# SwitchHead output gates: rows repeated from DRAM into 64 partitions and multiplied in place, instead of spread by TensorE products

## The chip, the cores and the metric

One core of a Trainium2 chip runs the whole program as one launch. The metric is the device time of that launch in microseconds (us). Engines are called by the names of the profile: PE (TensorE), PEld (its weight loads), DVE (VectorE), ACT (ScalarE), POOL (GpSimd) and SP, whose queue issues nearly all DMA transfers.

## What is computed

Four layers run one after the other on an input of 4 x 1024 x 128: two Mamba layers, SwitchHead attention with an FFN, a narrow attention, and a mixture of experts. The change is in the second. Its reference, cut to what matters (here H = 16 heads, P = 64, E = 8 experts, K = 2, D = 128; after the input is replaced, the batch is 4 and the length 1024):

```
def _gate(x, Wsel):
    s = jax.nn.sigmoid(jnp.einsum('bsd,hed->bhse', x, Wsel))
    _, idx = jax.lax.top_k(s, K)
    mask = jax.nn.one_hot(idx, E, dtype=s.dtype).sum(-2)
    return s * mask

q = _rope(einsum('bsd,hdp->bhsp', x, Wq)); k = _rope(einsum('bsd,hdp->bhsp', x, Wk))
gv = _gate(x, Wsel_v)
v = einsum('bsd,bhse,hedp->bhsp', x, gv, Wv)
att = softmax(einsum('bhsp,bhtp->bhst', q, k) / sqrt(P))
o = einsum('bhst,bhtp->bhsp', att, v)
go = _gate(x, Wsel_o)
return einsum('bhsp,bhse,hepd->bsd', o, go, Wo)
```

The last line is what the change is about: for each head and each of its 8 experts, the head's output `o` (64 features, transposed, so features lie on partitions) is multiplied by that expert's gate, one number for each position, and then by that expert's 64 x 128 matrix.

## The kernel before

**Tiling.** Heads go in pairs: 4 batches x 8 pairs = 32 pairs, and each pair in two halves of 512 positions. Head 0 of the pair lies on partitions 0 to 63, head 1 on 64 to 127. The work of a pair is spread over 8 "turns", so that the stage has 64 x 4 = 256 turns and some more at its end.

**A turn.** `turn` writes the steps of all engines in one list; every engine runs through this list in order and does its own part of each step, with semaphores between the engines. Turn m (d = m % 8) holds for PE: two `col` steps (transposed scores of this pair, which ACT turns into exponentials), two `row` steps (scores of the next pair, of which DVE takes the maximum), `bcast`, two `values` steps (products of the exponentials with V), at times `sums` (column sums of the exponentials, added up before on POOL) and `qk` (the projection of the pair after next, in turns d = 0 and 2), `onto`, one piece of the next batch's gates or of the FFN of the batch before (`ahead`: `prelude`, `ffn`, in the last batch `tables` and `decay`), at times `max_t`, and `v` (the value projection, which DVE multiplies by the value gates and sums over experts). DVE ends a turn with `recip`, a reciprocal of a quarter of the sums.

**PSUM.** The steps of PE that other engines read share a ring of three slots of 128 x 1024 in the order of the list: a step waits until the slot used three ring steps before has been read.

**The output gates.** `gate_t` transposes the gates of 512 positions to one row for each head and expert. ACT and DVE split them into three bf16 parts (`gate_mid`, `gate_res`, `gate_lo`), `gate_store` writes them to DRAM, and with `out_weights` SP brings the 16 rows of the pair, three parts, back twice into the tile `GS` (48 of each 64 partitions). `bcast` (L1387 to L1395) multiplies a constant selection matrix `selg` by `GS`: two products of 48 x 128 with 48 x 512, bf16, put the gates of two experts for both heads onto 128 partitions in PSUM. DVE multiplies this 128 x 1024 (L1727) by `OT`, the scaled output of the half, into `OG`, of which there are two; `onto` (L1404) multiplies `OG` by the experts' matrices and adds up in PSUM (`Z`); after four such steps, `collect` (L1740) adds `Z` to the batch's output. Unit x, one of 256 (half and expert pair), is in `bcast` in turn x + 9 and in `onto` in turn x + 10.

**`OT`** is made on POOL (L1944) at the end of turns d = 0 and 4, out of the head output that ACT has copied and the reciprocals. POOL also adds up the exponentials (L1953, L1956: seven additions of 128 x 1024 in four turns, two in most turns), does the rotary products of `qk` (L1918, after a transfer that swaps rows, and L1924), and parts of the search for the two largest gates (`top_a` to `top_d`) and of the FFN's affine steps.

**The end.** After the last `col` the remaining `values`, `sums`, `bcast` and `onto` steps follow one another closely, and `last_ffn` is woven in. One of its first steps is `d_load`, with which SP loads the first operands of the next layer.

Of the kernel before, what the change touches and what calls it, by code (L numbers as in the profile page):

```python
# [12 lines left out]
NB = 4  # L13
# [813 lines left out]
class SwitchHead:  # L827
    NORMS = 4

    def __init__(self, nc, ctx, room, c, W):  # L830
# [13 lines left out]
        self.selg = sb("selg", [128, 8, 128], BF16)  # L844
# [9 lines left out]
        self.GS = [sb(f"GS{u}", [128, L], BF16) for u in range(2)]  # L854
# [5 lines left out]
        self.OG = [sb(f"OG{u}", [128, 2, 512]) for u in range(2)]  # L860
# [12 lines left out]
        self.gt_d = dram("s_gt", (2, 3, 128, L), BF16)  # L873
# [5 lines left out]
        self.RG = self.TT[:, 0:512]  # L879
# [7 lines left out]
        ring = ("rows", "gate", "gate_t", "qk", "v", "row", "max_t", "col", "sums", "bcast", "f_t", "f_rows",  # L887
# [6 lines left out]
        for name in ("consts_in", "selg_in", "selg_done", "zeroed", "ln_chain", "ln_out", "top_v", "own_top", "b2_done", "spill_out", "top_done", "gt_hi",  # L894
                     "gt_mid", "gt_res", "gt_lo", "gates_out", "gv_out", "raw_done", "swap_in", "turn_done",
                     "rope_done", "wq_in", "wv_in", "gvj_in", "v_done", "mm_done", "m_s", "m_v", "m_in", "values_done",
                     "add_done", "o_done", "recip_done", "ot_done", "gs_in", "wo_in", "onto_done", "outt_done", "wf_in", "xn_in", "aff_done",
                     "t_in", "t_s", "t_v", "ij_in", "d_f", "d_hi", "d_mid", "d_lo", "d_res"):
            self.__setattr__(name, ctx.enter_context(nc.semaphore("s_" + name)))

# [48 lines left out]
    def turn(self, m, rows, vs, ahead):  # L949
# [15 lines left out]
        if due(self.BCAST):  # L965
            h, e = part(self.BCAST)
            out.append(("bcast", *self.of_half(h), e))
# [6 lines left out]
        h, x = part(self.SUMS)  # L974
        if due(self.SUMS) and x == 0:
            out.append(("sums", *self.of_half(h)))
# [12 lines left out]
        if due(self.SUMS):  # L989
            out.append(("recip", *self.of_half(h), x))  # L990
# [146 lines left out]
    def sync(self, sp):  # L1137
# [5 lines left out]
        sp.dma_start(self.M1[:, 0:16], W["s_selg"]).then_inc(self.selg_in, 16)  # L1143
        sp.wait_ge(self.zeroed, 7)
        for step in self.steps:
# [6 lines left out]
            elif kind == "gate_store":  # L1152
                if b > 1:
                    sp.wait_ge(self.gs_in, 96 * 8 * (b - 1))
                sp.wait_ge(self.gt_lo, 2 * (b + 1))
                for p in range(3):
                    sp.dma_start(self.gt_d[b % 2, p], self.GT[:, p, :]).then_inc(self.gates_out, 16)
# [41 lines left out]
            elif kind == "out_weights":  # L1199
                j, k = step[2], self.turns(*step[1:])  # L1200
                if k > 1:
                    sp.wait_ge(self.onto_done, 8 * (k - 1))
                    r.taken(sp, ("bcast", *self.pair(k - 2), 1, 3))
                if k:
                    sp.wait_ge(self.wo_in, 16 * k)
                    sp.wait_ge(self.gs_in, 96 * k)
# [4 lines left out]
                sp.wait_ge(self.gates_out, 48 * (b + 1))  # L1211
                for p in range(3):
                    for at in (16 * p, 64 + 16 * p):
                        sp.dma_start(self.GS[j % 2][at:at + 16, :],
                                     self.gt_d[b % 2, p, 16 * j:16 * j + 16, :]).then_inc(self.gs_in, 16)
            elif kind == "f_load":
                if b + 2 < NB:
                    sp.wait_ge(self.gates_out, 48 * (b + 3))
                    r.filled(sp, ("gate_t", b + 2, 1))
# [72 lines left out]
    def tensor(self, pe):  # L1292
        c, r, n = self.c, self.r, self.n
        for step in self.steps:
# [3 lines left out]
            if kind == "consts":  # L1298
                pe.wait_ge(self.consts_in, 16 * 5)
                pe.wait_ge(self.selg_done, 1)  # L1300
                pe.wait_ge(self.zeroed, 7)
# [156 lines left out]
    def scalar(self, s):  # L1458
        c, r, n = self.c, self.r, self.n
        for step in self.steps:  # L1460
# [18 lines left out]
            elif kind == "consts":  # L1479
                s.wait_ge(self.selg_in, 16)  # L1480
                s.activation(self.selg[:, :, :].rearrange("p e (h m) -> p (e h) m", h=2), bcast(self.M1[:, 0:16], 64),
                             ACT.Copy).then_inc(self.selg_done, 1)
                s.wait_ge(self.consts_in, 16 * 5)
                s.wait_ge(self.zeroed, 7)
# [11 lines left out]
            elif kind == "gate_t":  # L1496
                r.filled(s, step)
                if b > 0:
                    s.wait_ge(self.gates_out, 48 * b)
                s.activation(self.GT[:, 0, 512 * j:512 * j + 512], ps[:, 0:512], ACT.Copy).then_inc(self.gt_hi, 1)  # L1500
            elif kind == "gate_mid":
                r.taken(s, ("gate_t", b, j))
# [1540 lines left out]
```

## Time and profile before

| what | value |
|---|---|
| median of 3 runs | 5604.74 us (5603.9 to 5605.07) |
| time of the profiled execution | 5603.34 us |
| its span in the profile | 5601.5 us |
| PE busy | 5008.6 us (89%) |
| DVE busy | 4141.8 us (74%) |
| POOL busy | 2670.9 us (48%) |
| ACT busy | 2434.5 us (43%) |
| granted PE clock, mean | 0.965 of full |
| bytes moved by DMA | 340.14 MB |

The busy times are shares of the whole span, over stages with different limits. The stage of this change runs from about 1023 us (the end of Mamba) to 3945 us. Instructions are pipelined, so that the distance from one start to the next says more than a duration does.

### The profile page before, as it was taken

The numbers are of one execution on the slowest core, as the hardware profiler recorded it, in microseconds if no ns is written. First come the engines' busy times: TensorE is split into PE (matmuls) and PEld (weight loads), VectorE is DVE, ScalarE is ACT, GpSimd is POOL, SyncE is SP. The second block draws the span as 40 slices with busy tenths as digits, with TensorE's granted clock in tenths as the row PEclk, the third lists the DMA queues.
The fourth block names the chain that finished last, engine by engine and source line by source line (L and its number), as shares of the span: only waits on it lengthen the run. The fifth ranks groups of instructions, "written<-read, shape, count | busy, mean of one in ns | idle before, by whom it ended". The sixth has DMA issues, their size and how long they took to land.

```text
span 5601.5 us, 69295 instructions
## 1 busy us (share of the span) xinstructions
PE 5008.6 (89%) x23700; PEld 1998.6 (36%) x23738; DVE 4141.8 (74%) x4659; ACT 2434.5 (43%) x2991; POOL 2670.9 (48%) x1431
## 2 busy tenths in 40 slices
PE   7898998699999999999999999999788888888756
PEld 3333333233333333433334333433333322222225
DVE  5889989777777777677776787675777788888721
ACT  5655555133222323323233222332356656777753
POOL 4887888466655665556655555554211110110015
PEclk9999999899999999999999999999799999999978
DMA  4555555210110101101011011011121111011005
GB/s 149 180 188 180 188 190 191 72 38 23 36 33 23 30 24 42 33 23 30 23 44 33 24 35 34 23 42 21 45 42 41 36 22 30 24 29 19 2 12 177
DMA packets 137560, 340.14 MB, mean 61 GB/s; under 512 B 31867, under 2 KB 48766, under 8 KB 136564
## 3 DMA queue, kind: packets, MB, share of 16 engines
q1 hardware_dynamic: 134216, 329.40, 19.8%
q0 software_dynamic: 3008, 6.32, 0.3%
q8 instruction: 204, 3.34, 0.2%
q14 instruction: 132, 1.08, 0.1%
HBM read 289.59 MB, written 35.04 MB: 58 GB/s over the span
## 4 chain that ended last, share of the span: by engine, by line
PE 37%; issue 8%; DVE 4%; ACT 3%; POOL 1%; SPq 0%; POOLq 0%; DMA 0%; ACTq 0%; DVEq 0%
PE ps L2310 7%; PE ps L1377 4%; PE ps L1404 4%; PE ps L1362 3%; PE ps L1349 3%; PE ps L2281 3%; PE ps L1340 3%; PE ps L2263 3%; ACT n_P L2368 2%; DVE n_MX L2446 1%; PE ps L1366 1%; PE ps L2710 1%; PE ps L2721 1%; PE ps L2214 1%; PE ps L1333 1%
## 5 line engine op out<-in xcount | busy, mean ns | idle before, releaser
L2446 DVE TENSOR_REDUCE n_MX<-ps 128x2 f32<-128x1024 f32 (+7 forms) x1040 | 980.0, 975 | 223.5 <-PE ps L2263 128.8
L1956 POOL TENSOR_TENSOR s_PA<-s_PA,shared 128x1024 f32<-128x1024 f32 x384 | 908.8, 2367 | 318.0 <-ACT shared L1532 290.2
L1532 ACT ACTIVATE shared<-ps 128x1024 f32<-128x1024 f32 x512 | 522.1, 1022 | 1127.0 <-PE ps L1366 1114.6
L2368 ACT ACTIVATE n_P<-ps 128x1024 f32<-128x1024 f32 (+4 forms) x1021 | 823.0, 838 | 401.5 <-PE ps L2281 210.6
L767 POOL TENSOR_TENSOR m_PR<-m_HH,m_CS 128x1024 f32<-128x1024 f32 x256 | 606.0, 2383 | 162.5 <-issue 146.9
L1698 DVE TENSOR_REDUCE s_MX<-ps 128x2 f32<-128x1024 f32 x512 | 592.7, 1201 | 5.0 <-PE ps L1349 4.7
L1690 DVE TENSOR_TENSOR XTB<-ps,s_GVJ 128x1024 f32<-128x1024 f32 x256 | 312.9, 1222 | 358.6 <-PE ps L1340 356.6
L1349 PE MATMUL ps<-s_QF 64*128 64x512 f32 x2048 | 500.8, 606 | 71.5 <-DVE XTB L1690 44.7
L1362 PE MATMUL ps<-s_QF 64*128 64x512 f32 x2048 | 553.5, 617 | 6.9 <-DVE s_MX L1698 4.7
L2310 PE MATMUL ps<-n_P,n_VA 128*32 128x512 f32 (+3 forms) x3584 | 518.6, 577 | 17.4 <-ACT n_P L2368 17.0
L544 PE MATMUL ps<-m_PR,ident 128*128 128x512 f32 x1024 | 506.3, 622 | 11.0 <-DVE m_ZS L736 6.4
L1404 PE MATMUL ps<-s_OG,s_WO 128*128 128x512 f32 x1024 | 501.9, 612 | 0.7 <-DVE s_OUTT L1740 0.5
L1377 PE MATMUL ps<-shared,s_V 128*64 128x512 f32 x2048 | 496.8, 606 | 0.0
L1340 PE MATMUL ps<-s_WV,XTB 128*128 128x512 f32 x1024 | 482.7, 594 | 1.3 <-DVE XTB L1690 0.8
L730 DVE TENSOR_TENSOR_SCAN m_HH<-m_DA,ps 128x1024 f32<-128x1024 f32 x176 | 402.5, 2287 | 6.6 <-ACT m_DA L666 0.6
L1727 DVE TENSOR_TENSOR s_OG<-ps,s_OT 128x1024 f32<-128x1024 f32 x256 | 311.1, 1215 | 90.8 <-issue 60.8
L1918 POOL TENSOR_TENSOR s_TA<-s_TA,s_CS 128x1024 f32<-128x1024 f32 x64 | 151.3, 2364 | 472.8 <-DMA s_TA<-XTB 472.8
L2493 POOL TENSOR_TENSOR ln_small<-ln_small,n_half 128x8 f32<-128x8 f32 x11 | 18.1, 1648 | 641.0 <-DVE ln_small L2405 641.0
L1692 DVE TENSOR_REDUCE s_V<-XTB 128x128 f32<-128x1024 f32 x256 | 312.4, 1220 | 8.8
L1349 PEld LDWEIGHTS ps<-s_QF 64*128 64x128 f32 x2048 | 200.8, 190 | 303.7 <-issue 274.1
L1404 PEld LDWEIGHTS ps<-s_OG,s_WO 128*128 128x128 f32 x1024 | 178.1, 189 | 307.8 <-issue 304.6
L1362 PEld LDWEIGHTS ps<-s_QF 64*128 64x128 f32 x2048 | 177.4, 186 | 290.6 <-issue 285.1
(372 smaller groups left out, 7102.4 us busy)
## 6 DMA issues: line engine op xcount, KB each, us to landing
m_CS<-m_rows_c SPq DMA_DIRECT2D x256, 512.0 KB
m_BS<-m_rows_c SPq DMA_DIRECT2D x80, 512.0 KB
s_WV<-in_s_v SPq DMA_DIRECT2D x32, 512.0 KB, 3.7
s_TA<-XTB SPq DMA_DIRECT2D x256, 64.0 KB, 2.3
s_WO<-in_s_o SPq DMA_DIRECT2D x32, 512.0 KB, 3.9
g_WB<-in_g_wx SPq DMA_DIRECT2D x23, 578.0 KB
n_parts<-n_PT SPq DMA_DIRECT2D x14, 768.0 KB, 3.3
shared<-n_parts SPq DMA_DIRECT2D x144, 64.0 KB
```

Of the source, the lines that this page charges most:

```text
L767: g.tensor_tensor(self.PR[n % 4][:, :], self.HH[n % 4][:, :], self.CS[n % self.NCS][:, :], ALU.mult).then_inc(self.prod_done, 1)
L1340: ins = pe.matmul(ps[:, q], self.xt(b)[:, t * 128:(t + 1) * 128], self.WV[:, q], start=True, stop=True)
L1349: ins = pe.matmul(ps[:, 512 * h:512 * h + 512], QF[hs, 0, t * 128:(t + 1) * 128], QF[hs, 1, 512 * q:512 * q + 512], start=True, stop=True)
L1362: pe.matmul(ps[:, 512 * h:512 * h + 512], QF[hs, 1, t * 128:(t + 1) * 128], QF[hs, 0, qs], start=True, stop=False)
L1377: ins = pe.matmul(self.O[64 * h:64 * h + 64, :], self.V[j % 2][:, h, t, :], self.P[g % 4][:, 512 * h:512 * h + 512], start=t == 0, stop=t ...
L1404: ins = pe.matmul(self.Z, self.WO[j % 2][:, 2 * e + i, :], self.OG[e % 2][:, i, :], start=e == i == 0, stop=e == 3 and i == 1)
L1532: s.activation(self.P[g % 4], ps, ACT.Exp).then_inc(*r.take(step))
L1698: v.tensor_reduce(self.MX[:, q, :, t], ps.rearrange("p (h n) -> p h n", h=2), AX.X, ALU.max, negate=True).then_inc(*r.take(step))
L1956: g.tensor_tensor(PA, PA, P, ALU.add).then_inc(self.add_done, 1)
L2310: ins = pe.matmul(ob[at:at + 32, lo - 512 * q:512], self.VA[s % 3][:, t, 8 * g + 2 * hp + hh, :], self.P[(32 * n + 8 * hp + t) % 3][q][:, ...
L2368: ins = s.activation(P[:, at:at + x.shape[1], lo:512], x[:, :, lo:512], ACT.Exp, scale=scale)
L2446: ins = v.tensor_reduce(self.MX[:, q, at:at + x.shape[1], hp, t], x[:, :, 0:width], AX.X, ALU.max)
```

## The change

- The gate rows are kept as one f32 row for each head and expert (`GTF`, in the place of `GT`). `gate_t` is copied by ACT alone; the splitting into three parts, with `gate_mid`, `gate_res` and `gate_lo`, is gone, and so are `selg`, `GS` and their setup.
- A new step `gate_in`, one for each unit x, in turn x + 7 behind `onto`: SP loads for each of the two heads the two rows of 512 gates, repeated onto 64 partitions, into `OG` itself, of which there are now three (NG = 3). Before that it waits until `onto` x - 3 is done.
- The two products of `bcast` are gone, and the step leaves the PSUM ring. In its place in the list stands `gated`: `OG` is multiplied by `OT` in place, on DVE for even x (even expert pairs, odd turns) and on POOL for odd x (even turns).
- `onto` waits for the one or the other, and POOL's `OT` step for both.

```diff
@@ order
-            out.append(("bcast", *self.of_half(h), e))
+            out.append(("gated", *self.of_half(h), e))
...
         if due(self.BCAST + 1):
             ho, eo = part(self.BCAST + 1)
             out.append(("onto", *self.of_half(ho), eo))
             if eo == 3:
                 out.append(("collect", *self.of_half(ho)))
+        if 0 <= m - self.BCAST + 2 < 64 * NB:
+            h, e = part(self.BCAST - 2)
+            out.append(("gate_in", *self.of_half(h), e))
...
     def gate_pieces(self, b, r):
-        for kind in ("gate_t", "gate_mid", "gate_res"):
-            self.out.append((kind, b, r))
-            yield
-        self.out.append(("gate_lo", b, r))
+        self.out.append(("gate_t", b, r))
+        yield
@@ SP
+            elif kind == "gate_in":
+                j, q, e = step[2:]
+                x = 4 * self.half(b, j, q) + e
+                if x >= self.NG:
+                    sp.wait_ge(self.onto_done, x - self.NG + 1)
+                sp.wait_ge(self.gates_out, 16 * (b + 1))
+                for h in range(2):
+                    at = 16 * j + 8 * h + 2 * e
+                    src = self.gt_d[b % 2, at:at + 2, 512 * q:512 * q + 512]
+                    sp.dma_start(self.OG[x % self.NG][64 * h:64 * h + 64, :, :],
+                                 src.partition_broadcast(64)).then_inc(self.og_in[x % self.NG], 16)
@@ SP, out_weights
-                sp.wait_ge(self.gates_out, 48 * (b + 1))
-                for p in range(3):
-                    for at in (16 * p, 64 + 16 * p):
-                        sp.dma_start(self.GS[j % 2][at:at + 16, :],
-                                     self.gt_d[b % 2, p, 16 * j:16 * j + 16, :]).then_inc(self.gs_in, 16)
@@ PE
-            elif kind == "bcast":
-                q, e = step[3:]
-                pe.wait_ge(self.gs_in, 96 * (self.turns(b, j) + 1))
-                r.empty(pe, step)
-                for i in range(2):
-                    rows = slice(64 * i, 64 * i + 48)
-                    ins = pe.matmul(ps[:, 512 * i:512 * i + 512], self.selg[rows, 2 * e + i, :],
-                                    self.GS[j % 2][rows, 512 * q:512 * q + 512], start=True, stop=True)
-                ins.then_inc(*r.fill(step))
@@ PE, onto
-                r.taken(pe, ("bcast", *step[1:]))
+                x = 4 * self.half(b, j, q) + e
+                pe.wait_ge(self.og_g if e % 2 else self.og_v, x // 2 + 1)
...
-                    ins = pe.matmul(self.Z, self.WO[j % 2][:, 2 * e + i, :], self.OG[e % 2][:, i, :],
+                    ins = pe.matmul(self.Z, self.WO[j % 2][:, 2 * e + i, :], self.OG[x % self.NG][:, i, :],
@@ DVE
-                v.tensor_tensor(self.OG[e % 2][:, :, :], ps.rearrange("p (i n) -> p i n", i=2),
-                                self.OT[k % 2][:, :].unsqueeze(1).to_broadcast([128, 2, 512]),
-                                ALU.mult).then_inc(*r.take(step))
+            elif kind == "gated" and step[4] % 2 == 0:
+                self.gated(v, step, self.og_v)
...
+    def gated(self, e, step, done):
+        k = self.half(*step[1:4])
+        x = 4 * k + step[4]
+        OG = self.OG[x % self.NG][:, :, :]
+        e.wait_ge(self.og_in[x % self.NG], 32 * (x // self.NG + 1))
+        e.wait_ge(self.ot_done, k + 1)
+        e.tensor_tensor(OG, OG, self.OT[k % 2][:, :].unsqueeze(1).to_broadcast([128, 2, 512]), ALU.mult).then_inc(done, 1)
@@ POOL
+            elif step[0] == "gated" and step[4] % 2:
+                self.gated(g, step, self.og_g)
```

## Rows read from the trace of the kernel before

**Rows 1.** Busy time by stretch of the stage: engines, granted PE clock, DMA share, GB/s.
```profile
1612.00:2314.00 702.00, 694.16 (x2716) 275.18 (x2714) 512.39 (x529) 206.41 (x266) 395.55 (x195) 1.00 0.11 30
...
3885.00:3911.00 26.00, 23.49 (x66) 8.11 (x64) 19.04 (x34) 4.33 (x8) 2.53 (x2) 1.00 0.51 78
3911.00:3946.00 35.00, 17.26 (x110) 14.90 (x112) 16.43 (x62) 12.78 (x35) 0.23 (x1) 0.90 0.00 1
```

**Rows 2.** Timeline of PE in a turn: start us, us, engine line, out<-in.
```profile
2421.55 1.88 PE L1349 MATMUL ps<-s_QF 64*128 64x512 f32 x8
2423.26 0.39 PE L1394 MATMUL ps<-s_GS,s_selg 48*128 48x512 bf16 x2
2423.58 1.94 PE L1377 MATMUL ps<-shared,s_V 128*64 128x512 f32 x8
```

**Rows 3.** Timeline of PE in a turn before the first gate product.
```profile
1196.46 1.88 PE L1349 MATMUL ps<-s_QF 64*128 64x512 f32 x8
...
1198.28 1.94 PE L1377 MATMUL ps<-shared,s_V 128*64 128x512 f32 x8
```

**Rows 4.** Part 5 of the page: DVE's multiplications by value gates and output gates.
```profile
L1690 DVE TENSOR_TENSOR XTB<-ps,s_GVJ 128x1024 f32<-128x1024 f32 x256 | 312.9, 1222 | 358.6 <-PE ps L1340 356.6
...
L1727 DVE TENSOR_TENSOR s_OG<-ps,s_OT 128x1024 f32<-128x1024 f32 x256 | 311.1, 1215 | 90.8 <-issue 60.8
```

**Rows 5.** Timeline of all engines, turn 1 of a pair (2431 to 2442 us).
```profile
2432.78 2.35 POOL L1918 TENSOR_TENSOR s_TA<-s_TA,s_CS 128x1024 f32<-128x1024 f32 x1 [7.57 <-DMA s_TA<-XTB]
...
2438.75 4.85 POOL L1956 TENSOR_TENSOR s_PA<-s_PA,shared 128x1024 f32<-128x1024 f32 x2
2438.89 1.23 DVE L1727 TENSOR_TENSOR s_OG<-ps,s_OT 128x1024 f32<-128x1024 f32 x1 [2.41 <-issue]
...
2440.03 0.68 DVE L1740 TENSOR_TENSOR s_OUTT<-s_OUTT,ps 128x512 f32<-128x512 f32 x1
...
2441.54 1.23 DVE L1690 TENSOR_TENSOR XTB<-ps,s_GVJ 128x1024 f32<-128x1024 f32 x1 [0.83 <-PE ps L1340]
...
2443.68 1.88 PE L1349 MATMUL ps<-s_QF 64*128 64x512 f32 x8
```

**Rows 6.** Timelines of POOL, DVE and PE, turn 5 of the same pair.
```profile
2477.24 4.86 POOL L1956 TENSOR_TENSOR s_PA<-s_PA,shared 128x1024 f32<-128x1024 f32 x2
...
2478.41 1.22 DVE L1708 TENSOR_TENSOR s_MM<-s_MX 128x16 f32<-128x16 f32 x1 [0.23 <-DVE s_MX L1698]
2479.55 1.21 DVE L1727 TENSOR_TENSOR s_OG<-ps,s_OT 128x1024 f32<-128x1024 f32 x1
...
2483.35 1.23 DVE L1690 TENSOR_TENSOR XTB<-ps,s_GVJ 128x1024 f32<-128x1024 f32 x1
...
2485.50 1.88 PE L1349 MATMUL ps<-s_QF 64*128 64x512 f32 x8
```

**Rows 7.** Timelines: DVE with two SBUF inputs, POOL idle and POOL working.
```profile
1087.77 0.17 DVE L1708 TENSOR_TENSOR s_MM<-s_MX 128x16 f32<-128x16 f32 x1
...
3312.08 12.22 POOL L1956 TENSOR_TENSOR s_PA<-s_PA,shared 128x1024 f32<-128x1024 f32 x4
...
3315.55 6.54 DVE L1824 SCALAR_TENSOR_TENSOR Y<-Y 128x1024 f32<-128x1024 f32 x2
```

**Rows 8.** Timelines of DVE and PE, a turn 1 that carries a search piece.
```profile
1311.36 2.80 DVE L1627 TENSOR_TENSOR s_TG<-s_TG,s_M 128x512 f32<-128x512 f32 x1
...
1315.44 1.99 PE L1349 MATMUL ps<-s_QF 64*128 64x512 f32 x8 [2.74 <-DVE XTB L1690]
```

**Rows 9.** DMA issues: size of each, median us from issue to landing.
```profile
s_WO<-in_s_o SPq DMA_DIRECT2D x32, 512.0 KB, 3.9
```

**Rows 10.** Timeline of PE and SP at the end of the stage.
```profile
3884.95 1.98 PE L1404 MATMUL ps<-s_OG,s_WO 128*128 128x512 f32 x4
...
3887.26 8.21 SPq L824 DMA_DIRECT2D shared<-n_parts  x24
...
3908.54 1.96 PE L1404 MATMUL ps<-s_OG,s_WO 128*128 128x512 f32 x4 [0.17 <-DVE s_OG L1727]
```

More of the change, by code:

```diff
@@ L828 @@
     NORMS = 4
+    NG = 3
     def __init__(self, nc, ctx, room, c, W):
@@ L859, in __init__ @@
         self.OT = [sb(f"OT{u}", [128, 512]) for u in range(2)]
-        self.OG = [sb(f"OG{u}", [128, 2, 512]) for u in range(2)]
+        self.OG = [sb(f"OG{u}", [128, 2, 512]) for u in range(self.NG)]
         self.PA = [sb(f"PA{u}", [128, L]) for u in range(2)]
@@ L886, in __init__ @@
         self.O, self.Z = PS[:, 3072:3584], PS[:, 3584:4096]
-        ring = ("rows", "gate", "gate_t", "qk", "v", "row", "max_t", "col", "sums", "bcast", "f_t", "f_rows",
+        ring = ("rows", "gate", "gate_t", "qk", "v", "row", "max_t", "col", "sums", "f_t", "f_rows",
                 "f_up", "f_down", "d_rows", "d_qk", "d_qk2", "d_v")
@@ L973, in turn @@
                     out.append(("keep", *self.pair(k), i // 8))
-        h, x = part(self.SUMS)
+        hs, x = part(self.SUMS)
         if due(self.SUMS) and x == 0:
-            out.append(("sums", *self.of_half(h)))
+            out.append(("sums", *self.of_half(hs)))
         if d in (0, 2):
@@ L1152, in sync @@
             elif kind == "gate_store":
-                if b > 1:
-                    sp.wait_ge(self.gs_in, 96 * 8 * (b - 1))
-                sp.wait_ge(self.gt_lo, 2 * (b + 1))
-                for p in range(3):
-                    sp.dma_start(self.gt_d[b % 2, p], self.GT[:, p, :]).then_inc(self.gates_out, 16)
+                for u in range(self.NG if b > 1 else 0):
+                    sp.wait_ge(self.og_in[u], 32 * len(range(u, 64 * (b - 1), self.NG)))
+                for x in range(2):
+                    r.taken(sp, ("gate_t", b, x))
+                sp.dma_start(self.gt_d[b % 2], self.GTF).then_inc(self.gates_out, 16)
+            elif kind == "gate_in":
[9 more added lines that the diff above has]
+                                 src.partition_broadcast(64)).then_inc(self.og_in[x % self.NG], 16)
             elif kind == "gv_store":
@@ L1210, in sync @@
                     sp.dma_start(c.slots[at, :], W["g_blank"]).then_inc(c.blank, 16)
[L1211 to L1215 removed]
             elif kind == "f_load":
                 if b + 2 < NB:
[L1218 to L1219 removed]
+                    sp.wait_ge(self.gates_out, 16 * (b + 3))
                     sp.wait_ge(self.top_done, self.tops(b + 2))
@@ L1498, in scalar @@
                 if b > 0:
[L1499 to L1502, printed above, removed]
-                s.activation(self.GT[:, 1, 512 * j:512 * j + 512], self.RG, ACT.Copy).then_inc(self.gt_mid, 1)
-            elif kind == "gate_lo":
-                s.wait_ge(self.gt_res, 2 * b + j + 1)
-                s.activation(self.GT[:, 2, 512 * j:512 * j + 512], self.RG, ACT.Copy).then_inc(self.gt_lo, 1)
+                    s.wait_ge(self.gates_out, 16 * b)
+                s.activation(self.GTF[:, 512 * j:512 * j + 512], ps[:, 0:512], ACT.Copy).then_inc(*r.take(step))
             elif kind == "qk":
@@ L1544, in scalar @@
                 r.filled(s, step)
-                if j == 0 and b + 2 < NB:
-                    s.wait_ge(self.gt_res, 2 * (b + 3))
                 s.activation(self.TT[:, j % 2 * 256:(j % 2 + 1) * 256], ps[:, 0:256], ACT.Copy).then_inc(*r.take(step))
@@ L1900, in gpsimd @@
         self.own_p = own = Own(g, self.c.own_g)
-        for u in range(2):
-            g.memset(self.GS[u][:, :].bitcast(F32), 0.0).then_inc(self.zeroed, 1)
         g.memset(self.TA[:, 1, :], 0.0).then_inc(self.zeroed, 1)
@@ L1942, in gpsimd @@
                 if k > 1:
-                    self.r.taken(g, ("bcast", *self.pair((k - 2) // 2), k % 2, 3))
+                    g.wait_ge(self.og_v, 2 * (k - 1))
+                    g.wait_ge(self.og_g, 2 * (k - 1))
                 g.tensor_tensor(self.OT[k % 2][:, :], self.OR[k % 2][:, 0, :], self.OR[k % 2][:, 1, :],
```

49 lines of the change are left out of this document (11 added, 38 removed).

## The prediction

> **What bounds the kernel now.** I read three views, in this order. First the busy time by stretch over the stage that the change touches [rows 1]: between 1612 and 3885 us TensorE (PE) is busy 99% of the time at the full granted clock, VectorE (DVE) 73%, GpSimd (POOL) 56%, the DMA engines 11%. The reader is to see that what leaves PE's queue shortens the stage, and that the other engines matter only where PE waits for them. Second, PE's timeline inside a turn, for what a piece costs from start to start; the mean durations in the groups overlap and overstate it. Third, the timelines of DVE, POOL and SP beside PE's, for the slack between each engine and the PE instruction that waits for it. The stage is 256 turns of 9.8 to 11.5 us.
>
> **PE: what goes.** With a gate product, the score rows ("row") start at 2421.55, the gate product at 2423.26 and the value products at 2423.58: 2.03 us from rows to values [rows 2]. Before the first gate product of the phase the same step takes 1198.28 - 1196.46 = 1.82 us [rows 3]. So one turn is worth 0.21 us, not the 2 x 378 ns that two products seem to take. Of 256, nine stand in the tail, which I price as a whole below: 247 x 0.21 = 52 us. Behind it in a ring of three PSUM slots, `row` still takes the slot that the last `v` of the turn before used, three places back as now; no slot gets tighter.
>
> **Small pieces.** The splitting of the gate rows into three bf16 parts (two copies on ScalarE and two subtractions on DVE each, eight times) goes, and so do DVE's multiplications of the even-numbered turns (half of 256, 1215 ns each, [rows 4]), which relieves DVE there. PE waits there only rarely; with the shorter start of the phase I allow 7 us of gain (0 to 12).
>
> **The new multiplications on POOL.** 128 of them, about 2.4 us each (half of the 4.85 us of two additions, [rows 5]). They fall in turns 0, 2, 4 and 6 of eight. In turn 0 POOL stands idle 7.57 us for the rotary swap's DMA [rows 5], which covers one; PE asks for the product a turn later. Cost nothing there; if that cover went, `ot` (the scaled head output) would be late.
>
> **The new multiplications on DVE.** Here is the main cost. Today the operand comes from PSUM. Afterwards both inputs are in SBUF. What such an instruction meets while POOL works is shown [rows 7]: the minimum of two 128x16 tiles takes 0.17 us with POOL idle, but 1.22 us at 2478.41 [rows 6], ending just as POOL's first addition does; and at 3315 two `scalar_tensor_tensor` take 6.54 us while POOL's four additions stretch to 12.22 us. They take turns, one whole instruction each. So a DVE multiplication waits for the POOL instruction in progress. DVE waits for PE before the `v` multiplication for 356.6 us in all, 1.4 a turn [rows 4]; in turns 3 and 7, with nothing else to do, for longer, and that covers it. Turns 1 and 5 carry more:
>
> Turn 1 [rows 5]: POOL starts its additions at 2438.75, the moment `ot` is done; DVE comes at 2438.89. It would wait to 2441.2 and end at about 2442.3 instead of 2440.12. Then come the collect (0.6 from start to start) and the `v` multiplication (1.23), which ends at 2444.1; PE's next row needs it. That row stands at 2443.68 and would come 0.21 earlier, 2443.47; with a handover of 0.1 (at 1311.36 DVE's 2.80 plus one `v` of 1.2 end at 1315.3, and PE starts at 1315.44, [rows 8]) PE loses 0.7 us. Bounds 0.4 to 0.9. 32 pairs: 22 us.
>
> Turn 5 [rows 6]: the 128x16 instruction slips in between POOL's two additions, and the multiplication follows at 2479.55 while POOL's second is due at 2479.65. If POOL gets in first, DVE waits to 2482.1 and ends at 2483.2, 2.4 later than now; 0.75 of that is idle today, so `v` ends 1.7 later, at 2486.3, against 2485.29 for PE: 1.0 us lost. If DVE gets in first, nothing or 0.3. The two are 0.1 us apart; in [rows 7] POOL always got in between two DVE instructions, but these waited for one another and this pair doesn't. I take the middle, 0.65: 21 us (5 to 32).
>
> The Trainium skill ("SBUF — State Buffer", Who interferes with whom) states the lock as a rule: a DVE instruction with two SBUF inputs contends with a GpSimd instruction that reads SBUF, and whichever starts first keeps the port for its whole length. The traces agree with the first half; by the second half alone DVE, which starts 0.1 us sooner, would win in turn 5, and the sum would be 16 us lower: that is the first rival.
>
> **Turns that also carry the top-2 search, the FFN or the tables.** PE already stalls there: 2.74 us before 1315.44, behind a DVE instruction of half the size that POOL held to 2.80 us [rows 8]. The later multiplication adds about 0.4 in such a turn 1 and 0.6 in a turn 3 (six each) and some in the table stretch: 8 us (3 to 18, as POOL has little left there).
>
> **SP's queue.** `gate_in` waits for the `onto` of its own turn, so SP now walks beside PE. Behind it stand the swap transfers, the maxima's six small transfers and the weights, each of which waits today for something of about the same place. A 512 KB load lands 3.9 us after issue [rows 9]; `gate_in` has some 17 us until its multiplication. 256 x 512 KB is 134 MB, 50 GB/s more on engines that are 11% busy. Nothing, in the steady part.
>
> **The tail is different.** Once the columns end (3884.95 to the last `onto` at 3908.54 plus 1.9, [rows 10]) each `gate_in` waits for the `onto` three back, then 4.3 us to land, then 1.2 (DVE) or 2.4 us (POOL), then 1.8 for `onto`: about 9 us for three. The loads of the next phase (`d_load`, 30 transfers, 24 of them in 8.21 us, 10.3 in all [rows 10]) stand between the last two `gate_in`s in SP's order. Counting from the end of the `onto` at 3884.95 (number 246 of 0 to 255) at 3886.9: load 249 issues at 0.1, lands at 4.4, POOL is done at 6.8 and `onto` 249 at 8.7. Load 250 issues after `onto` 247 (2.9) and its `onto` ends at 10.5; load 251, after `onto` 248 (5.5), lands at 9.8, POOL 12.2, `onto` 14.1. Loads 252 to 254 so issue at 8.8, 10.6 and 14.2, and `onto` 252, behind `ot`, a collect and four transposes, ends at 18.2. `d_load` then runs to 25.2; load 255 lands at 29.5, is multiplied to 32, and its `onto` ends at 33.7, against 23.5 today. 10 us, and as PE would be half busy for as long as from 3911 to 3946, where the granted clock was 0.90 [rows 1], 3 more: 13 us (6 to 20).
>
> The Trainium skill ("SBUF — State Buffer", Door 1: The DMA port swizzle) says that a transfer onto 64 partitions reaches only half the SBUF ports, and that two of them serialize. By its 196 GB/s an estimate for the two halves is 2.7 us of transfer, which would put some 1 to 2 us on a landing and about 4 us on the tail; no row here shows such a transfer.
>
> **Sum.** -52 - 7 + 22 + 21 + 8 + 13 = +5 us. The profiled execution took 5603.34 (span 5601.5), 1.4 under the median 5604.74. 5603.3 + 5 = 5608. A change of 0.2%, 11 us, is about what a measurement of this kernel tells from none; so I forecast no measurable change: PE's gain is given back by waits for DVE.
>
> **Rivals.**
>
> *The lock hardly reaches PE (faster).* DVE wins turn 5 (5 instead of 21), and turn 1 costs 0.4 (13): -52 - 7 + 13 + 5 + 5 + 10 = -26, 5577. For it: the 0.1 us lead at 2479.55. Against it: POOL's start at 2438.75 is plain, and turn 1's slack is only some 0.8 us.
>
> *POOL always first, and POOL short of time (slower).* Turn 5 at 32 us, turn 1 at 26, the search turns at 18, the tail at 17, relief 3: -52 - 3 + 26 + 32 + 18 + 17 = +38, 5641. The mechanism is one, the port shared by DVE and POOL; it decides from about 1.9 us of PE stall in eight turns, where the 1.7 us saved are gone (the rest being the tail). For it: the alternation at 3312, and POOL, which would be busy nearly all of turns 0 to 3 during the search.
>
> *The rows come late in every turn (much slower).* If a `gate_in` were held behind another wait of SP for more than some 13 us, PE would stand at each `onto`; at 0.3 us in each of 256 turns 77 us, 5680. Against it: none of SP's waits, ordered as PE runs, is that long.
>
> *The products cost PE nothing, so that nothing is gained (slower too).* Against it: [rows 2, 3]. I give it no more than 0.02, inside the slower ones.
>
> **Chances.** No measurable change 0.33; first rival 0.32; slower by the lock 0.29; slower by late rows or otherwise 0.06. Faster by over 0.2%: 0.32; within: 0.33; slower: 0.35. Range for 8 in 10: from 5574 (first rival with its bounds) to 5640; the likeliest case's own is 5593 to 5616.
>
> **What would show it.** In the changed profile: no matmul from the gate rows, rows to values 1.82 us; DVE's multiplications with a mean near 2 us instead of 1.215, those of turn 1 ending 3.5 us after `ot`; PE stalls of some 0.5 to 1 us before the `row` of turns 2 and 6, some 60 of them, put down to the `v` multiplication; POOL's multiplications near 2.4 us; the last `onto` about 34 us after the columns end, behind a `gate_in` issued after the 24 loads. I am wrong if stalls appear at `onto` itself in the steady part (rows late), if DVE's mean stays at 1.2 us (no lock), or if turns 2 and 6 start on time.

## The result, and the profile after

The changed kernel takes 5641.68 us (median of 4 runs, 5634.91 to 5650.98) beside 5604.90 (4 runs of before, 5603.90 to 5613.09): a ratio of 1.0064, 95% interval 1.005 to 1.0079. That is 37 us slower, 34 over the predicted 5608, and 1.7 above the upper end of the range. The profiled execution, the fastest of the four, took 5634.91, span 5633.1, which is 31.6 over the span of before; I account for those 31.6.

The page and the windows first: groups of part 5 that answer to [rows 4], and two issues that answer to [rows 9].

```profile
L1663 DVE TENSOR_TENSOR XTB<-ps,s_GVJ 128x1024 f32<-128x1024 f32 x256 | 312.2, 1220 | 316.1 <-PE ps L1341 315.0
L1745 DVE TENSOR_TENSOR s_OG<-s_OG,s_OT 128x1024 f32<-128x1024 f32 x128 | 297.1, 2321 | 118.0 <-POOL s_OT L1920 110.5 <-DMA s_OG<-s_gt 7.5
L1745 POOL TENSOR_TENSOR s_OG<-s_OG,s_OT 128x1024 f32<-128x1024 f32 x128 | 308.9, 2414 | 33.3 <-DMA s_OG<-s_gt 33.3
...
s_OG<-s_gt SPq DMA_DIRECT2D x512, 256.0 KB, 3.9
...
s_WO<-in_s_o SPq DMA_DIRECT2D x32, 512.0 KB, 5.1
```

DVE's new multiplication takes 2.32 us in the mean where 1.2 is its own work, as forecast; POOL's takes 2.41. A transfer of gate rows lands 3.9 us after its own issue. Each multiplication needs two, of which the second is issued 0.6 us behind the first, and the pair has landed 4.75 us after the first issue (median of the 256 pairs), where I took 4.3. The neighbouring weights land 1.2 us later than before, and no wait of PE is put down to them. By stretch [rows 1]:

```profile
1612.00:2314.00 702.00, 683.17 (x2579) 266.52 (x2579) 517.47 (x507) 205.82 (x260) 490.96 (x228) 0.99 0.28 75
...
3910.00:3978.00 68.00, 26.26 (x125) 17.88 (x124) 22.13 (x80) 14.63 (x40) 3.63 (x2) 0.77 0.26 45
```

PE is busy 97% of the middle of the stage where it was 99%; POOL went from 56% to 70%, the DMA engines from 11% to 28%. The end of the stage has become 68 us in which PE mostly stands, at a granted clock of 0.77.

**Where the 31.6 us are.** In both traces I take from PE's timeline the start of the value products of every turn, 250 starts, of which the last lies at the end of the columns; then the start of the next phase's first product (out of `shared`); then the end of the span.

| | before | after | difference |
|---|---|---|---|
| the last of these value products starts at | 3878.98 | 3884.81 | +5.8 |
| from there to the next phase's first product | 66.8 | 93.6 | +26.8 |
| from there to the end of the span | 1655.7 | 1654.7 | -1.0 |

The first line contains -2.8 from ahead of the first of these turns (in the ten kernels below it is between -2.3 and +0.6, so no more than a fluctuation need be in it). Of the 249 intervals behind it 160 are shorter by 0.19 to 0.24 us. The others differ by what PE waits in them; most are longer, but 24 are shorter by more than that, up to 3.0 us, since before had a wait there too. Counting 0.215 for each of the 249 as gained (53.5 in all), PE's waits cost 62.2 us more than they did before. By the place of the turn in its eight, this net cost lies so:

| turn | 1 | 3 | 5 | the other five |
|---|---|---|---|---|
| us lost, sum over all pairs | 30.3 | 20.5 | 4.5 | 6.9 |

A blocked multiplication is not yet a loss: in turn 7, one of the other five, DVE's takes 2.8 us in 28 of the 32 pairs, and PE loses 3.6 us there in all.

**Turn 1**, the pair of [rows 5], in the timelines of POOL, DVE and PE after:

```profile
2438.30 8.14 POOL L1932 TENSOR_TENSOR s_PA<-s_PA,shared 128x1024 f32<-128x1024 f32 x3
...
2438.45 3.28 DVE L1745 TENSOR_TENSOR s_OG<-s_OG,s_OT 128x1024 f32<-128x1024 f32 x1 [2.43 <-POOL s_OT L1920]
2441.65 0.68 DVE L1706 TENSOR_TENSOR s_OUTT<-s_OUTT,ps 128x512 f32<-128x512 f32 x1
2442.25 1.21 DVE L1663 TENSOR_TENSOR XTB<-ps,s_GVJ 128x1024 f32<-128x1024 f32 x1
...
2443.61 1.99 PE L1350 MATMUL ps<-s_QF 64*128 64x512 f32 x8 [0.43 <-DVE XTB L1663]
```

POOL starts its additions 0.15 us ahead of DVE, DVE waits one whole addition out, and the `v` multiplication behind it ends 0.15 before PE's late row. The interval is 0.70 longer than a stall-free one would be: the predicted 0.7.

**Turn 5** of the same pair [rows 6]:

```profile
2476.61 5.73 POOL L1932 TENSOR_TENSOR s_PA<-s_PA,shared 128x1024 f32<-128x1024 f32 x2
...
2477.78 1.23 DVE L1681 TENSOR_TENSOR s_MM<-s_MX 128x16 f32<-128x16 f32 x1 [0.23 <-DVE s_MX L1671]
2478.93 1.21 DVE L1745 TENSOR_TENSOR s_OG<-s_OG,s_OT 128x1024 f32<-128x1024 f32 x1
...
2483.14 1.21 DVE L1663 TENSOR_TENSOR XTB<-ps,s_GVJ 128x1024 f32<-128x1024 f32 x1
...
2484.65 1.88 PE L1350 MATMUL ps<-s_QF 64*128 64x512 f32 x8
```

The multiplication takes its bare 1.21 us right behind the 128x16 instruction, and it is POOL that waits: its two additions take 5.73 us instead of 4.86. PE doesn't wait. The Trainium skill's rule ("SBUF — State Buffer", Who interferes with whom: the one that starts first holds the port for its whole instruction) fits both turns.

**The end of the stage** [rows 10], the timelines of SP, POOL and PE:

```profile
3909.69 0.72 SPq L812 DMA_DIRECT2D shared<-in_n_ones  x2
3910.45 1.55 SPq L817 DMA_DIRECT2D shared<-n_pieces  x4
3912.05 8.21 SPq L824 DMA_DIRECT2D shared<-n_parts  x24
3920.35 1.23 SPq L1166 DMA_DIRECT2D s_OG<-s_gt  x2
...
3936.87 2.34 POOL L1745 TENSOR_TENSOR s_OG<-s_OG,s_OT 128x1024 f32<-128x1024 f32 x1 [25.57 <-DMA s_OG<-s_gt]
...
3939.35 3.75 PE L1397 MATMUL ps<-s_OG,s_WO 128*128 128x512 f32 x4 [22.74 <-POOL s_OG L1745]
```

The order is the predicted one, `gate_in` 255 behind the 30 loads. But its rows have all landed only 16.5 us after issue (3920.35 to 3936.8), not 4.3, and then PE does its four products at half speed, 3.75 us for the 1.96 of [rows 10]. By the semaphore's events 16 of the pair's 32 completions come by 3926.8, and the other 16 between 3935.2 and 3936.8. The last issue ends at 3921.6, yet the DMA engines are still busy in the stretch between, at a share of 0.61 and 99 GB/s, while PE stands at half clock:

```profile
3924.00:3934.00 10.00, 0.00 (x0) 0.00 (x0) 0.00 (x0) 0.00 (x0) 0.00 (x0) 0.50 0.61 99
```

That is 1 MB in 10 us, twice what the pair itself moves, so the loads ahead were still moving after the last of them had been issued. From 3937 on the share is 0.00.

### The profile page after: what moved, and what is told of

The parts are those of the page before. It is cut to its first block and busy times, and to the rows that moved or that the text cites. A ratio compares the mean times of both kernels' runs of the same rounds, so it can differ in the third digit from the quotient of the medians.

```text
span 5633.1 us, 68612 instructions
## 1 busy us (share of the span) xinstructions
PE 4978.9 (88%) x23226; PEld 1969.7 (35%) x23226; DVE 4150.7 (74%) x4515; ACT 2423.8 (43%) x2974; POOL 3056.8 (54%) x1557
## 5 line engine op out<-in xcount | busy, mean ns | idle before, releaser
L1932 POOL TENSOR_TENSOR s_PA<-s_PA,shared 128x1024 f32<-128x1024 f32 x384 | 981.3, 2555 | 197.8 <-ACT shared L1516 167.3
L1350 PE MATMUL ps<-s_QF 64*128 64x512 f32 x2048 | 513.3, 618 | 108.7 <-DVE XTB L1663 81.5
L1363 PE MATMUL ps<-s_QF 64*128 64x512 f32 x2048 | 554.6, 618 | 6.4 <-DVE s_MX L1671 4.6
L1745 DVE TENSOR_TENSOR s_OG<-s_OG,s_OT 128x1024 f32<-128x1024 f32 x128 | 297.1, 2321 | 118.0 <-POOL s_OT L1920 110.5
L1745 POOL TENSOR_TENSOR s_OG<-s_OG,s_OT 128x1024 f32<-128x1024 f32 x128 | 308.9, 2414 | 33.3 <-DMA s_OG<-s_gt 33.3
L1350 PEld LDWEIGHTS ps<-s_QF 64*128 64x128 f32 x2048 | 203.5, 193 | 350.2 <-issue 321.0
```

The costliest lines, as they stand in the source:

```text
L1350: ins = pe.matmul(ps[:, 512 * h:512 * h + 512], QF[hs, 0, t * 128:(t + 1) * 128], QF[hs, 1, 512 * q:512 * q + 512], start=True, stop=True)
L1363: pe.matmul(ps[:, 512 * h:512 * h + 512], QF[hs, 1, t * 128:(t + 1) * 128], QF[hs, 0, qs], start=True, stop=False)
L1745: e.tensor_tensor(OG, OG, self.OT[k % 2][:, :].unsqueeze(1).to_broadcast([128, 2, 512]), ALU.mult).then_inc(done, 1)
L1932: g.tensor_tensor(PA, PA, P, ALU.add).then_inc(self.add_done, 1)
```

## The experiments

Each ratio is to the kernel before as it was measured beside that kernel; its median was 5604.9 us beside the kernel after and 5608.1 to 5610.5 beside the ten others, so that a difference in us to the kernel after can be off by 3 to 6 us where the ratios are not. "Waits" is what PE's waits cost over the 249 turns beyond those of before, "end" the time from the last of these turns to the next phase beyond the 66.8 us of before; both are from one trace each, worked out as above. After, e2 and e9 have the same schedule in these turns and show 62.2, 68.9 and 61.7, so a difference of 7 in "waits" needs no cause. The rest of the program takes 1653 to 1658 us in all of them but e10 (1662) and e12 (1664), and why it does in these two is open.

| kernel | us | ratio, 95% | waits | end |
|---|---|---|---|---|
| after | 5641.7 | 1.0064 (1.0050 to 1.0079) | 62.2 | 26.8 |
| e1 places kept | 5652.5 | 1.0079 (1.0063 to 1.0096) | 72.3 | 33.9 |
| e2 loads last | 5623.9 | 1.0026 (1.0016 to 1.0035) | 68.9 | 7.2 |
| e8 one SBUF input on DVE | 5594.4 | 0.9984 (0.9973 to 0.9995) | 15.0 | 27.9 |
| e9 no rows | 5610.4 | 1.0002 (0.9992 to 1.0012) | 61.7 | -2.4 |
| e3 all on POOL | 5668.0 | 1.0105 (1.0090 to 1.0121) | 84.2 | 34.7 |
| e4 all on DVE | 5647.2 | 1.0073 (1.0058 to 1.0089) | 74.3 | 24.6 |
| e5 DVE's behind `v` | 5600.8 | 0.9986 (0.9977 to 0.9995) | 18.6 | 32.9 |
| e6 both repairs | 5582.7 | 0.9956 (0.9942 to 0.9969) | 19.0 | 14.6 |
| e10 e6, all on DVE | 5587.8 | 0.9961 (0.9948 to 0.9973) | 29.2 | 4.4 |
| e12 e6, places kept | 5586.5 | 0.9956 (0.9939 to 0.9972) | 18.9 | 14.4 |

**e1: the pieces' places.** The removed splitting pieces had each used up a turn of the list of extra work, so that the search's second half and the FFN now come two and four turns sooner.

```
             yield from self.gate_pieces(b, r)
+            yield
+            yield
```

> The kernel after, with two empty places behind each gate_t of batches 1 to 3, where the splitting pieces stood: the pieces behind them (the second half of the search, the FFN) go back to the turns that they have in the kernel before. Theory (part of the loss is not the lock but these pieces coming four turns sooner, the FFN's two affine products on POOL into the turn in which POOL also makes the rotary product and sum): the 13.4 us that turns 88 to 111 and 152 to 175 lose beyond the 0.215 a turn shrink to under 4, and the whole is 8 to 14 us faster than the kernel after, 5628 to 5634. Rival (places do not matter, the search and the FFN lose what they lose to the lock): within 3 us of the kernel after.

Both fell: nothing came back. By the medians it is 11 us slower still, but the intervals of the two ratios overlap. The traces show more. The turns 96 to 103 and 160 to 167 do get back what I meant, 12.0 us each (the FFN's first affine products are no longer in the turn of POOL's rotary ones, where after PE waited 2.75 us for them). But the turns 88 to 95 and 152 to 159 lose 5 us each by the move, and 112 to 119 and 176 to 183 lose 11, since the FFN's last norm now meets a turn 1. DVE, then PE, in e1:

```profile
2349.78 3.28 DVE L1747 TENSOR_TENSOR s_OG<-s_OG,s_OT 128x1024 f32<-128x1024 f32 x1 [2.51 <-POOL s_OT L1922]
...
2353.80 1.49 DVE L791 TENSOR_TENSOR ln_small<-ln_small 128x8 f32<-128x8 f32 x1
2355.33 0.17 DVE L793 TENSOR_TENSOR ln_small<-ln_small 128x8 f32<-128x8 f32 x1
2355.53 2.25 DVE L795 TENSOR_SCALAR ln_small<-ln_small 128x8 f32<-128x8 f32 x1
2357.81 0.17 DVE L797 TENSOR_TENSOR ln_small<-ln_small 128x8 f32<-128x8 f32 x1
2358.01 2.24 DVE L799 SCALAR_TENSOR_TENSOR ln_small<-ln_mean_var,ln_small 128x8 f32<-128x8 f32 x1
2360.18 1.21 DVE L1665 TENSOR_TENSOR XTB<-ps,s_GVJ 128x1024 f32<-128x1024 f32 x1
...
2361.53 3.78 PE L1352 MATMUL ps<-s_QF 64*128 64x512 f32 x8 [7.11 <-DVE XTB L1665]
```

Instructions on 8 numbers a partition, 0.17 us each, take 1.5 to 2.25 us wherever one of POOL's additions got in between; POOL was at four additions in a row just then. One of those held up, L795, has a single SBUF tensor as its input. PE stands 7.11 us. So what a place costs depends on which pieces stand with a blocked multiplication ahead of `v`.

**e2: the 30 loads behind the last `gate_in`.**

```
-        for piece in ([("f_t", b, 0), ("d_load", 0)], norm("f_ln1", 0)[:2], ...
+        for piece in ([("f_t", b, 0)], [("d_load", 0)] + norm("f_ln1", 0)[:2], ...
```

> The kernel after, with the 30 loads of the next phase behind the last gate_in in SP's order. Theory (the last gate rows take 16.5 us to land because 24 loads stand in the DMA queues ahead of them): they land within 5 us of issue, the last onto starts some 20 us sooner, and the whole is 15 to 22 us faster than the kernel after, about 5621. Rival (gate rows onto 64 partitions land slowly in the tail by themselves): the landing stays over 10 us and the time within 5 us of the kernel after. Second rival: the tail shortens but the next phase then waits for its own loads, and less than half of the 20 us is left.

As the theory has it: 19.6 us of the 26.8 at the end are gone (26.8 to 7.2), and the next phase does not wait for its loads: it starts 35.9 us behind the start of the last `onto`'s last matmul, in this kernel as in before. The time itself is 18 us below after. SP and POOL:

```profile
3908.80 15.21 SPq L1166 DMA_DIRECT2D s_OG<-s_gt  x10
3924.12 0.72 SPq L812 DMA_DIRECT2D shared<-in_n_ones  x2
...
3928.33 2.74 POOL L1745 TENSOR_TENSOR s_OG<-s_OG,s_OT 128x1024 f32<-128x1024 f32 x1 [7.40 <-DMA s_OG<-s_gt]
```

The last pair of row transfers begins at 3922.8 (3908.80 + 15.21 less the 1.2 us that a pair takes to issue) and POOL starts on it 5.5 us later.

**e8: one SBUF input.** DVE's half is replaced by an instruction of the same length with one input; this kernel leaves the head outputs out of the even gate rows.

```
+        if one:
...
+            e.tensor_reduce(self.SC[:, :], OG, AX.X, ALU.max).then_inc(done, 1)
+            return
```

> The kernel after, but DVE's half of the gate multiplications (the even ones) is replaced by a maximum over the same 128x1024 tile: one SBUF input in place of two, of about the same 1.2 us; the even gate rows go to the output projection without the head outputs in them. Theory (the port shared by DVE and POOL costs PE the stalls behind turn 1's v multiplication and a share of those in the search): DVE's mean falls from 2.32 to about 1.2 us, turn 1 loses nothing in the plain pairs (0.7 us before), and the whole is 20 to 35 us faster than the kernel after, 5607 to 5622. Rival (DVE simply has more to do there, or POOL's own new products are what delays): the same stalls, within 6 us of the kernel after.

The waits fall from 62.2 to 15.0, more than I had put on it. Turn 1 loses nothing:

```profile
2424.60 1.22 DVE L1749 TENSOR_REDUCE s_SC<-s_OG 128x2 f32<-128x1024 f32 x1 [2.45 <-issue]
...
2424.47 7.35 POOL L1938 TENSOR_TENSOR s_PA<-s_PA,shared 128x1024 f32<-128x1024 f32 x3
...
2429.15 1.88 PE L1351 MATMUL ps<-s_QF 64*128 64x512 f32 x8
```

Both engines run side by side at full speed. What POOL's new products and DVE's own time cost without the port is within the 15.0 us that stay.

**e9: no transfers.** Only the first three loads of gate rows are made, and the head output is multiplied by itself; the gates of the output projection are left out.

```
                 if x >= self.NG:
-                    sp.wait_ge(self.onto_done, x - self.NG + 1)
+                    continue
...
-        e.tensor_tensor(OG, OG, self.OT..., ALU.mult)
+        e.tensor_tensor(OG, self.OT..., self.OT..., ALU.mult)
```

> The kernel after without the gate rows' transfers but the first three: both engines multiply the head output by itself instead, two SBUF inputs as now, and wait for the onto three back themselves; the gates of the output projection are left out of the computation. Theory (the transfers cost nothing in the steady part and about 26 us in the tail): turns keep their stalls, the last onto comes about 25 us sooner, the whole is 22 to 30 us faster, about 5614. Rival (transfers also slow other landings: weights 4.4 instead of 3.7 us, swaps): a further 5 to 20 us in the search turns.

The waits stay (61.7), the whole surplus at the end goes (-2.4). 134 MB more through the DMA engines cost the steady part nothing that a turn's length shows (227 of the 249 intervals agree with the kernel after to 0.1 us). The rival is right in that the row transfers slow others: without them the weights land after 3.9 us again, for 5.1 in the kernel after. But nothing waits for that.

**e3 and e4: who multiplies.** In each one engine does all 256 (`elif kind == "gated" and step[4] % 2 == 0` and its counterpart on POOL lose their condition or go).

> The kernel after with all 256 gate multiplications on POOL. POOL gets 128 x 2.41 = 309 us more (71% of the stage becomes 82%), DVE loses as much. Theory (what costs is a DVE multiplication waiting behind a POOL instruction): the turn 1 of a plain pair loses its 0.7 us no more, and the stage is 10 to 30 us shorter where POOL has time, some of it given back in the search and table turns: 5615 to 5640. Rival (POOL is short of time as well, and its instructions in turns 1 and 5, behind the head output, hold the additions and with them PE): slower than the kernel after by 10 us or more, with PE waiting for POOL's results or for ACT's, whose buffers POOL frees.

> The kernel after with all 256 gate multiplications on DVE. POOL is as busy as in the kernel before. Theory (the port): the second 128 multiplications wait for POOL's instruction too, in the turns that carry the rotary product and sum; DVE's mean stays above 2 us, and the time is 10 to 50 us above the kernel after, 5650 to 5690. Rival (POOL's load is what costs, by stretching its chains in the search turns): 10 us or more below it.

e3: slower than after by 26 us, so the time is the rival's, although the theory's own part holds (turn 1 of a plain pair, one without extra pieces, is 0.70 us shorter again). Over all pairs turn 1 gives 46 us back and turn 5 loses 47. In six of the ten plain pairs that loss is 1.36 us:

```profile
2490.57 2.48 DVE L1685 TENSOR_TENSOR s_MR<-s_MT,s_MS 16x128 f32<-16x128 f32 x1
...
2490.56 2.34 POOL L1745 TENSOR_TENSOR s_OG<-s_OG,s_OT 128x1024 f32<-128x1024 f32 x1
...
2495.05 1.99 PE L1350 MATMUL ps<-s_QF 64*128 64x512 f32 x8 [1.09 <-DVE XTB L1663]
```

It is the port again and not POOL's total time: POOL's multiplication starts 0.01 us ahead of the splitting of the maxima on DVE, which stands ahead of `v`, and 0.28 us (what this instruction took in nearly every pair before) become 2.48; it takes over 2 us in 18 of the 32 pairs. PE's waits for POOL's own results, the rival's sign, are 5.6 us, as in the kernel after (5.5). e4: 5.5 us slower than after by the medians, under the theory's 10 and not clear of noise; DVE's mean is 2.11 us, as expected above 2, and the waits are 12 us more. POOL's 309 us less give nothing that shows.

**e5: DVE's multiplication behind `v`.** One step changes place in the list: for even `e`, `gated` is emitted behind `next(vs, None)` and not ahead of the value products. `onto` of the next turn is what needs it.

> The kernel after with one order changed: DVE's gate multiplication stands behind the v multiplication of its turn instead of ahead of it. The port is shared as before; only what is queued behind the blocked instruction changes. Theory (the 47 us that a one-input instruction in its place gave back are the v multiplication being late behind it): the plain pairs' turn 1 loses nothing, and 25 to 45 us come back, 5597 to 5617. Rival (the block costs wherever it stands, since the score maxima behind it then free their slots late): within 10 us of the kernel after, with PE's waits put down to the maxima instead.

Inside what the theory gave: 41 us below after by the medians. DVE, POOL and PE in the turn 1 that stands above:

```profile
2418.53 1.23 DVE L1665 TENSOR_TENSOR XTB<-ps,s_GVJ 128x1024 f32<-128x1024 f32 x1 [1.03 <-PE ps L1343]
2419.79 1.22 DVE L1667 TENSOR_REDUCE s_V<-XTB 128x128 f32<-128x1024 f32 x1
2420.93 1.22 DVE L1747 TENSOR_TENSOR s_OG<-s_OG,s_OT 128x1024 f32<-128x1024 f32 x1
...
2420.91 3.45 POOL L1934 TENSOR_TENSOR s_PA<-s_PA,shared 128x1024 f32<-128x1024 f32 x1 [0.15 <-ACT shared L1518]
...
2420.68 1.88 PE L1352 MATMUL ps<-s_QF 64*128 64x512 f32 x8
```

The two still meet, here with POOL waiting (3.45 us for an addition of 2.35), but the `v` multiplication no longer stands behind. PE's waits between 1190 and 3880 us (total, times, longest), before, after and then e5:

```profile
PE ps L1349 <- DVE XTB L1690: 41.2, 30, 6.1
```

```profile
PE ps L1350 <- DVE XTB L1663: 78.0, 47, 9.5
```

```profile
PE ps L1352 <- DVE XTB L1665: 44.0, 39, 6.3
...
PE ps L1399 <- POOL s_OG L1747: 4.4, 4, 3.6
PE ps L1399 <- DVE s_OG L1747: 4.1, 4, 2.0
```

The waits for `v` are nearly back at those of before. New are 8.5 us of waits for the gate products themselves, which `onto` now finds late in some turns. And not only what stands behind has changed: the mean of DVE's multiplication fell from 2.32 to 1.53 us, so in its new place it is also blocked less. e10 below separates the two.

**e6: both repairs.**

> The two repairs together: DVE's gate multiplication behind the v multiplication, and the next phase's 30 loads behind the last gate_in. Theory: they add up, 25 to 45 and 18 us below the kernel after, 5579 to 5599, which is 7 to 27 us below the kernel before. Rival (they overlap, or the first is worth nothing): 5610 or more.

They add up: 5582.7 us, 0.44% below the kernel before. The end costs 14.6 instead of e2's 7.2. 4.5 us of the difference lie between the last `onto` and the next phase (40.4 for 35.9, counted as in e2), and there the clock was low: the FFN's first products, with the same instructions, in e6 and in e2:

```profile
3889.87 3.75 PE L1421 MATMUL ps<-s_TT,s_GT 128*128 128x256 f32 x8 [0.52 <-issue]
```

```profile
3935.34 1.97 PE L1419 MATMUL ps<-s_TT,s_GT 128*128 128x256 f32 x8 [0.52 <-issue]
```

The second is at 2.4 GHz, the first at 1.2 (granted clock 0.78 from 3872 to 3920 us in e6). Ahead of them PE had waited for the last gate rows' product 3.20 us in e6 and 3.72 in e2, so the length of that wait is not what tells them apart; why one fell and the other didn't, these rows don't show.

**e10 and e12** are e6 with one more change each: all multiplications on DVE, and e1's two places.

> The two repairs (DVE's gate multiplication behind the v multiplication, the 30 loads behind the last gate_in), and all 256 gate multiplications on DVE. Theory (with the order repaired a blocked DVE multiplication costs only its own time, and what stalls remain come from POOL's chains in the FFN and table turns): within 10 us of the two repairs alone, 5575 to 5593, with 5 to 10 us less lost in the FFN and table turns and some lost to DVE's fuller search turns. Rival (DVE's 128 more blocked multiplications of 2.3 us fill its slack): 15 us or more above it.

> The two repairs and the two empty places behind each gate_t of batches 1 to 3, which alone made the kernel after 11 us slower. Theory (what the places cost is which turns with a blocked DVE multiplication ahead of the v multiplication the search and FFN pieces meet, so with the order repaired they cost little): within 4 us of the two repairs alone, 5579 to 5587. Rival (the places cost by themselves, by POOL's FFN products meeting the rotary ones): 8 to 14 us above it, 5591 to 5597.

Both times are the theory's: 5587.8 and 5586.5. The places that alone went with 10 us more of waits (72.3 for 62.2) cost nothing with the order repaired (18.9 for 19.0). With all on DVE the waits are 10 us more (29.2), and not where I had put them: the FFN's turns (88 to 119 and 152 to 183) lose 11.9 us for 2.4 in e6, when they were to lose less, and only the tables' give 4 back. The end is 10 less. 5.6 of this lie ahead of the last `onto`, where no multiplication of 2.4 us stands in the chain any more; 4.5 lie behind it, where the clock did not fall as in e6 (35.9 us to the next phase for 40.4). e10 also answers the question left by e5: DVE is blocked there for 158 us in all (256 multiplications of 1.83 us instead of 1.21), more than the 142 of the kernel after (128 of 2.32), and PE's waits are 29.2 against 62.2.

## Why the prediction was wrong, point by point

The forecast was +5 and no measurable change; it came out at +31.6 in the profiled execution.

- **PE's gain, -52: right.** In 160 turns it shows by itself, 0.215; counted for all 249 it is 53.5. Of the 7 us allowed for relief and start no more than 2.8 can be seen.
- **DVE's wait behind POOL in turn 1: right in kind and size** (0.70 a plain pair). It was put at 0.7 in all 32 pairs, 22 us. Of the ten pairs without extra pieces that lie whole in these turns it comes in five; two have 0.07 and three of the last batch nothing, 3.8 us in all. Where search, FFN or tables run, turn 1 loses 27.0.
- **Turn 5, +21: wrong.** I took the middle between DVE first and POOL first. DVE was first in 30 of the 32 pairs, where its multiplication takes the bare 1.21 us right behind the 128x16 instruction, and POOL waited: 4.5 us for all pairs. The rows I had drawn the alternation from [rows 7] are of instructions that wait for one another; there POOL does get in each time. My own rival had this one right, and so had the rule of the Trainium skill ("SBUF — State Buffer", Who interferes with whom) cited beside it. The row of turn 6 starts on time, which I had named as a sign of being wrong.
- **Turns with search, FFN and tables, +8: mis-sized.** The 20 pairs with such pieces lose 57.6 of the 62.2 us (search 25.4, FFN 13.4, tables 18.8). My prices give them 20 x (0.7 + 0.65) + 8 = 35, and the other 12 pairs 16, where 4.6 are found. So the whole, 62.2 for 51, is nearer than its parts: 23 too little here, 12 too much there. I had costed one late multiplication a turn. What happens is in the timelines of DVE and PE in a search turn, which answer to [rows 8]:

```profile
1304.73 3.29 DVE L1745 TENSOR_TENSOR s_OG<-s_OG,s_OT 128x1024 f32<-128x1024 f32 x1 [3.61 <-POOL s_OT L1920]
...
1309.24 1.52 DVE L1608 TENSOR_TENSOR s_TG<-s_TG,s_M 128x512 f32<-128x512 f32 x1
1310.69 1.21 DVE L1663 TENSOR_TENSOR XTB<-ps,s_GVJ 128x1024 f32<-128x1024 f32 x1
...
1314.16 1.23 DVE L1671 TENSOR_REDUCE s_MX<-ps 128x2 f32<-128x1024 f32 x1
...
1312.05 3.58 PE L1350 MATMUL ps<-s_QF 64*128 64x512 f32 x8 [3.81 <-DVE XTB L1663]
```

  PE's wait grows by only 1.07 (3.81 for 2.74), but its row products, 1.99 us before, take 3.58; I read this as the maxima behind `v`, late too, handing back the slots late. The turn is 2.40 us longer than before, although the gate product is gone. The whole of DVE's queue is late, not one instruction.
- **The pieces' new places** I hadn't seen: removing two pieces moves all that follow. e1 has 10 us more of waits than the kernel after and 3 more than e2, so they helped the change by a few us; e12 shows that they are worth nothing once DVE's order is repaired.
- **The end, +13: wrong, +26.8.** The order was the forecast one: `gate_in` 255 is issued at 3920.35, as soon as the 24 loads are. Up to there the steps were sound: counted as in the forecast, `onto` 249 and 251 end at 9.2 and 15.5 (forecast 8.7 and 14.1), and load 255 is issued at 27.5 (25.2). The landing was taken from the steady part, 4.3 us; behind 24 loads of 64 KB it was 16.5, and the last `onto` ends at 50.3 and not at 33.7. e2, with the loads behind it, has 5.5, and e9, without rows, has no surplus. This is the step that failed: the landing of a transfer in a steady stretch was used for one that stands in a full queue. The 3 us allowed for a low clock behind the last `onto` did not come, 36.3 for the 35.9 of before. The estimate by the Trainium skill ("SBUF — State Buffer", Door 1: The DMA port swizzle), 1 to 2 us more on a landing for 64 partitions, is a little high for the steady part: a pair lands in 4.75 us where one load of 512 KB took 3.9 before, 0.85 more, of which 0.6 is the second one's later issue.
- **The rivals.** The nearest is "POOL always first, and POOL short of time", +38: its number is near and its mechanism, the shared port, is shown (e8: 47 of the 62 us of waits go with the second SBUF input). But half of its name is false: POOL wasn't first in turn 5, and its load as such costs nothing that shows (e4 relieves POOL of 309 us and gains nothing). "Late rows" can be excluded for the steady part by e9.

PE's waits are 1.94 us in eight turns (62.2 / 32), so they alone use up the 1.7 us gained there; nearly the whole loss is then the end.

Open: which of the loads ahead held the second half of the last rows' completions, while the first half came in 6.4 us, and whether e3's loss would go with another place for the splitting of the maxima; neither was tried. Nor was the repaired order in the kernel before, where each product waits in a PSUM slot that the `v` product of the same turn may need.

## What to carry to other kernels

A blocked instruction costs less by itself than by what stands behind it in its queue (e10 beside after). Before an operand moves from PSUM to SBUF, look for the engine that shares the port, and put the instruction behind everything that the bottleneck engine is about to ask for: that took 41 us off here, and with one more step moved made a loss of 37 into a gain of 25. Price a transfer near a phase's end by what stands ahead of it in the queue and not by its median, and when pieces leave a schedule written by turns, follow where the others land.

## What the hardware showed that I had not expected

- In these rows who gets the shared port goes with whether DVE's next instruction is ready. Back to back, DVE keeps it: at 2477.78 and 2478.93 two in a row, with POOL's second addition put off by 0.87 us. In a chain whose links wait for one another (e1, 2353.80 to 2360.18) POOL gets in at every second link and each time costs a 0.17 us instruction 1.3 to 2.1 us. One of the held links is a `tensor_scalar` with one SBUF tensor as input (2355.53), so two inputs are not a condition for every instruction.
- An instruction of 16x128 with two SBUF inputs took 2.48 us instead of 0.28 when POOL had started 0.01 us ahead (e3, 2490.57).
- A `tensor_reduce` of 128x1024 from SBUF ran its bare 1.22 us beside POOL's additions (e8), and these theirs: 2369 ns in the mean, as against 2555 in the kernel after.
- Two row transfers issued 8 us behind the first of 24 small loads had landed 16.5 us after issue, half of their completions after 6.4 and the rest after 14.8 to 16.5; the same two, ahead of the loads, 5.5 us.
